# Two-layer graph network on one core: the sums right of the diagonal are turned back in sweep 2 and joined there with the own term and the bias

## The reference, cut to what matters

```python
# layer 0
d = sum(adj, axis=1); s0 = 1 / (sqrt(d) + 1e-8)
x1 = layernorm(x + (adj * s0[:, None] * s0[None, :]) @ (x @ W0 + b0))
# layer 1
adj_hat = adj + eye; s1 = 1 / sqrt(sum(adj_hat, axis=1))
out = layernorm(x1 + relu((adj_hat * s1[:, None] * s1[None, :]) @ (x1 @ W1) + b1))
```

## Time and profile before

| | before |
|---|---|
| median of 3 runs (lowest, highest) | 1765.88 us (1765.54, 1769.53) |
| the profiled execution, its own time | 1766.01 us |
| its span | 1764.2 us |
| TensorE (PE) busy | 1651.8 us, 94% |
| VectorE (DVE) busy | 1057.1 us, 60% |
| ScalarE (ACT) busy | 751.1 us, 43% |
| GpSimd (POOL) busy | 148.7 us, 8% |
| granted TensorE clock, mean | 0.991 of full speed |

### The profile page before, as it was taken

How to read it: one execution, slowest core, us unless ns; L and a number is a source line. 1 busy time by engine, 2 the same in 40 slices (tenths; PEclk the granted TensorE clock), 3 DMA queues, 4 the chain that set the end, 5 groups by cost and what they waited for, 6 DMA issues and landing times.

```text
span 1764.2 us, 25751 instructions
## 1 busy us (share of the span) xinstructions
PE 1651.8 (94%) x10392; PEld 1475.7 (84%) x10392; DVE 1057.1 (60%) x1837; ACT 751.1 (43%) x900; POOL 148.7 (8%) x171
## 2 busy tenths in 40 slices
PE   0688989999999999989999999999999999999996
PEld 0678989999999999977888888888888888888885
DVE  2233234344444455487666666555556899999996
ACT  4332322232111000046455454445445777777773
POOL 0000000000000000121100000000001011111111
PEclk9999999999999999999999999999999999999998
DMA  9999999999999876347676766556566999999991
GB/s 385 421 420 421 420 421 411 420 414 421 401 409 386 328 301 255 111 171 292 247 268 238 251 248 240 208 221 240 202 236 280 420 419 419 399 386 388 393 397 68
DMA packets 85462, 572.41 MB, mean 324 GB/s; under 512 B 10304, under 2 KB 10560, under 8 KB 19808
## 3 DMA queue, kind: packets, MB, share of 16 engines
q1 hardware_dynamic: 76320, 541.23, 77.1%
q0 software_dynamic: 9024, 29.54, 4.6%
HBM read 556.03 MB, written 14.70 MB: 324 GB/s over the span
## 4 chain that ended last, share of the span: by engine, by line
PE 85%; DVE 6%; issue 3%; DMA 2%; ACT 1%; SPq 1%; POOL 0%; ACTq 0%; DVEq 0%; POOLq 0%
PE acc L742 37%; PE acc L775 15%; PE acc L777 15%; PE acc L776 15%; DVE low L897 3%; DMA lent<-adj_far 1%; SPq L593 1%; PE mixed L677 1%; ACT high L794 1%; DVE stats L875 1%; PE turned L686 1%; PE mixed L713 1%; PE acc L765 1%; DVE z L1056 0%; DMA x_in<-x_rows 0%
## 5 line engine op out<-in xcount | busy, mean ns | idle before, releaser
L775 PE MATMUL acc<-high,feat_high 128*128 128x512 f32 x1336 | 529.9, 397 | 6.9 <-DVE low L897 6.8
L777 PE MATMUL acc<-high,feat_low 128*128 128x512 f32 x1336 | 523.1, 392 | 0.0
L776 PE MATMUL acc<-low,feat_high 128*128 128x512 f32 x1336 | 522.9, 391 | 0.0
L897 DVE TENSOR_TENSOR low<-own,high 128x1024 fp32r<-128x1024 f32 x330 | 390.4, 1219 | 174.0 <-ACT high L794 172.4
L794 ACT CAST high<-own 128x1024 fp32r<-128x1024 f32 x330 | 335.6, 1052 | 173.9 <-PE acc L777 153.6
L742 PE MATMUL acc<-feat,lent 128*128 128x129 f32 x2880 | 334.1, 275 | 20.2 <-issue 13.8
L742 PEld LDWEIGHTS acc<-feat,lent 128*128 128x128 f32 x2880 | 327.5, 192 | 22.4 <-issue 15.8
L775 PEld LDWEIGHTS acc<-high,feat_high 128*128 128x128 f32 x1336 | 251.7, 188 | 63.0 <-issue 11.3
L777 PEld LDWEIGHTS acc<-high,feat_low 128*128 128x128 f32 x1336 | 251.3, 188 | 55.1
L776 PEld LDWEIGHTS acc<-low,feat_high 128*128 128x128 f32 x1336 | 251.7, 188 | 51.5
L897 DVE TENSOR_TENSOR low<-lent,high 128x1024 fp32r<-128x1024 f32 x182 | 211.8, 1218 | 8.4 <-ACT high L794 6.4
(11 more groups left out here) (90 smaller groups left out, 765.6 us busy)
## 6 DMA issues: line engine op xcount, KB each, us to landing
own<-adj_tiles SPq DMA_DIRECT2D x205, 1024.0 KB, 7.3
lent<-adj_tiles SPq DMA_DIRECT2D x181, 1024.0 KB, 11.0
lent_h<-adj_tiles SPq DMA_DIRECT2D x48, 1024.0 KB, 11.1
lent<-adj_far SPq DMA_DIRECT2D x41, 1024.0 KB, 15.7
own<-adj_far SPq DMA_DIRECT2D x20, 1024.0 KB, 13.8
lent_h<-adj_far SPq DMA_DIRECT2D x17, 1024.0 KB, 13.5
x_in<-x_rows POOLq DMA_DIRECT2D x32, 256.0 KB, 6.3
x_t<-x_cols SPq DMA_DIRECT2D x16, 256.0 KB, 10.9
```

The source lines that it names most:

```text
L775: nc.tensor.matmul(bank, f_high, a_high[:, chunk], start=(u == plan.first[g] and q == 0), stop=False)
L776: nc.tensor.matmul(bank, f_high, a_low[:, chunk], start=False, stop=False)
L777: mm = nc.tensor.matmul(bank, f_low, a_high[:, chunk], start=False, stop=(u == plan.last[g] and q == Q - 1))
L897: nc.vector.tensor_tensor(low(m), raw(n)[:, half * HALF:(half + 1) * HALF], high(m).bitcast(F32), ALU.subtract).then_inc(low_ready, 1)
```

## The change

- The own term leaves TensorE: VectorE makes `skip = scale_sq * mixed + b1` right behind `features1_low` of the row (new `add_own`; `scale_sq` is made once). The matmuls of L765 and the identity for them are gone.
- The right sums are not stored. TensorE turns them from `stage` into `turned` (new `turn_right`, 4 transposes), and VectorE adds them, scaled, to `skip` (new `add_right`). GpSimd's queue stores `skip` (`store_skip`, 16 times where 15 sums were stored) and loads it in sweep 3.
- `empty_left1` becomes a copy on ScalarE. `add_x1` adds `skip_in` instead of the bias.
- `AHEAD` of sweep 3 becomes 2, `turn_out` comes two takes later, `make_out` one take later.
- New waits: `turn0` waits for all `skip` of earlier rows, `turn1` for `own_added` of the rows before it.

```diff
-AHEAD = {1: 0, 2: 1, 3: 1}
+AHEAD = {1: 0, 2: 1, 3: 2}
...
+        self.turn_right = {i: max(self.features1[i] + 1, self.last[("right1", i)] + 2) for i in range(NB - 1)}
...
-            self.turn_out[i] = self.empty[g] + 1
+            self.turn_out[i] = self.empty[g] + 3
...
-            (act if g[0] in ("late0", "right1") else dve).append(
-                ((hi_key if g[0] in ("late0", "right1") else lo_key)(k, 1), "empty_" + g[0], g[1]))
-            if g[0] == "right1":
-                pool.append(((k, 2, 0), "store_right1", g[1]))
+            act.append((hi_key(k, 1), "empty_" + g[0], g[1]))
...
+            dve.append((lo_key(k2, 9), "add_own", i))
+            if i < NB - 1:
+                dve.append((lo_key(self.turn_right[i], 2), "add_right", i))
+            pool.append(((self.turn_right.get(i, k2 + 1), 6, 0), "store_skip", i))
...
-            act.append((hi_key(k + 2, 5), "make_out", i))
+            act.append((hi_key(k + 3, 5), "make_out", i))
...
+                if kind == "store_skip":
+                    pool.wait_ge(skip_ready, up(i) + 1)
+                    pool.dma_start(skip_rows[i], skip[:, up(i) % 2]).then_inc(skip_stored[up(i) % 2], 16)
...
                     elif kind == "turn0":
                         pe.wait_ge(h_ready, up(i))
+                        pe.wait_ge(skip_ready, up(i))
...
                             pe.wait_ge(feat1_ready, up(i))
+                            pe.wait_ge(own_added, up(i))
...
+                    elif kind == "turn_right":
+                        m = stage_at[("empty_right1", i)]
+                        pe.wait_ge(h_ready, up(i) + 1)
+                        pe.wait_ge(skip_ready, up(i))
+                        pe.wait_ge(staged, m + 1)
+                        for q in range(Q):
+                            mm = nc.tensor.transpose(turned_q[:, q, :], stage[:, m % 2, q * P:(q + 1) * P], ident[:, :])
+                        mm.then_inc(turn_right_done, 1)
...
-                    if half == 1 and u == plan.last.get(("left1", i)):
-
-                        bank = acc[plan.bank[("left1", i)]]
-                        for q in range(Q):
-                            for f in (feat_high[1], feat_low[1]):
-                                nc.tensor.matmul(bank[:, q * P:(q + 1) * P], f[:, i * Q + q, :], ident_r[:, :],
-                                                 start=False, stop=False,
-                                                 skip_group_check=True)
...
+                elif kind == "empty_left1":
...
+                    nc.scalar.copy(y_t[:, m % 2, :], acc[b][:, :]).then_inc(bank_emptied[b], 1)
...
+                elif kind == "add_own":
...
+                    if up(i) >= 2:
+                        dve.wait_ge(skip_stored[r], 16 * (up(i) // 2))
+                    dve.wait_ge(mixed1_done, up(i) + 1)
+                    for q in range(Q):
+                        ins = nc.vector.scalar_tensor_tensor(
+                            out=skip[:, r, q, :], in0=mixed_q[:, q, :], scalar=scale_sq[:, i, q:q + 1],
+                            in1=b_sb[:, :], op0=ALU.mult, op1=ALU.add)
+                    ins.then_inc(own_added, 1)
...
+                elif kind == "add_right":
+                    r = up(i) % 2
+                    dve.wait_ge(own_added, up(i) + 1)
+                    dve.wait_ge(turn_right_done, stage_at[("empty_right1", i)] + 1)
+                    for q in range(Q):
+                        ins = nc.vector.scalar_tensor_tensor(
+                            out=skip[:, r, q, :], in0=turned_q[:, q, :], scalar=scale[:, i, 1, q:q + 1],
+                            in1=skip[:, r, q, :], op0=ALU.mult, op1=ALU.add)
+                    ins.then_inc(skip_ready, 1)
```

More of the change, by code:

```diff
@@ L178, in __init__ @@
             self.features1[i] = min(self.turn1[i] + FEATURES1_LAG, need)
+        self.turn_right = {i: max(self.features1[i] + 1, self.last[("right1", i)] + 2) for i in range(NB - 1)}
+        assert all(self.turn_right[i] <= self.turn0[i - 1] for i in range(1, NB - 1) if i - 1 in self.late_rows)
         self.empty = {g: u + 1 for g, u in self.last.items()}
@@ L186, in __init__ @@
                 self.empty[g] = max(self.empty[g], self.turn_out[ROWS3[m - 2]])
-            self.turn_out[i] = self.empty[g] + 1
+            self.turn_out[i] = self.empty[g] + 3
             if m >= 1:
                 self.turn_out[i] = max(self.turn_out[i], self.turn_out[ROWS3[m - 1]] + 2)
-        for table, kind in ((self.turn0, "turn0"), (self.turn1, "turn1"), (self.features1, "features1")):
+        for table, kind in ((self.turn_right, "turn_right"), (self.turn0, "turn0"), (self.turn1, "turn1"),
+                            (self.features1, "features1")):
             for i in reversed(range(NB)):
-                if kind != "turn0" or i in self.late_rows:
+                if i in table and (kind != "turn0" or i in self.late_rows):
                     self.pe_before.setdefault(min(table[i], self.end), []).append((kind, i))
@@ L448, in gnn_kernel @@
         ident = put("ident", [P, P])
-        ident_r = put("ident_r", [P, P], F32R)
+        skip = put("skip", [P, 2, Q, P])
+        scale_sq = put("scale_sq", [P, NB, Q])
         ones = put("ones", [P, 1])
@@ L522, in gnn_kernel @@
         staged = sem("staged")
-        sums_stored = [sem(f"sums_stored{r}") for r in range(2)]
+        scale_sq_ready = sem("scale_sq_ready")
+        turn_right_done = sem("turn_right_done")
+        own_added = sem("own_added")
+        skip_ready = sem("skip_ready")
+        skip_stored = [sem(f"skip_stored{r}") for r in range(2)]
         sums0_ready = sem("sums0_ready")
@@ L563, in ring_of_x1 @@
             before = ring_of_x(0 if up(0) % 2 == r else 1)[1]
-            loaded = sum(16 * (2 if k != NB - 1 else 1) for k in ROWS3[:third[i] + 1] if third[k] % 2 == r)
+            loaded = sum(32 for k in ROWS3[:third[i] + 1] if third[k] % 2 == r)
             return r, before + loaded
@@ L831, in _ @@
                     act.sem_inc(sums0_ready, 1)
+                elif kind == "empty_left1":
+                    g = ("left1", i)
+                    b, m = plan.bank[g], third[i]
+                    act.wait_ge(halves_used, 2 * plan.last[g] + 2)
+                    if m >= 2:
+                        act.wait_ge(turn_out_done, m - 1)
+                    nc.scalar.copy(y_t[:, m % 2, :], acc[b][:, :]).then_inc(bank_emptied[b], 1)
+                    act.wait_ge(bank_emptied[b], plan.bank_turn[g] + 1)
+                    act.sem_inc(y_t_ready, 1)
                 elif kind == "make_out":
@@ L837, in _ @@
                     else:
-                        for r in range(2):
-                            act.wait_ge(sums_stored[r], 16 * len([k for k in stage_at.values() if k % 2 == r]))
+                        act.wait_ge(turn_right_done, NB - 1)
                     for q in range(Q):
@@ L978, in _ @@
                     ins.then_inc(feat0_ready, 1)
+                    if i == NB - 1:
+                        nc.vector.tensor_tensor(scale_sq[:, :, :], scale[:, :, 1, :], scale[:, :, 1, :],
+                                                ALU.mult).then_inc(scale_sq_ready, 1)
                 elif kind == "split_low":
@@ L1098 @@
     args.append(nc.dram_tensor("x1_rows", (NB, P, Q, P), F32, kind="Internal").ap())
-    args.append(nc.dram_tensor("sums_rows", (NB, P, T), F32, kind="Internal").ap())
+    args.append(nc.dram_tensor("skip_rows", (NB, P, Q, P), F32, kind="Internal").ap())
     args.append(nc.dram_tensor("nat_rows", (SPILLED, P, Q, W), F32, kind="Internal").ap())
```

49 lines of the change are left out of this document (15 added, 34 removed).

## The result

| | before | changed |
|---|---|---|
| median of the runs | 1767.13 us (6 runs, 1765.54 to 1771.34) | 1775.5 us (6 runs, 1772.75 to 1778.78) |
| ratio to before, with its 95% interval | | 1.0049 (1.0039 to 1.0059) |
| the profiled execution, and its span | 1766.01 us, 1764.2 | 1777.69 us, 1775.9 |
| granted TensorE clock, mean | 0.991 | 0.982 |

The six runs of before include the three known earlier. The change makes the kernel 8.4 us (0.5%) slower, where 10.1 was forecast.

What follows compares the result with a forecast made beforehand. TensorE bounds sweeps 2 and 3, except sweep 2's start, bound by a chain through GpSimd's load, VectorE and a tile load. 10.3 + 7.5 + 4.8 - 14.2 + 1.0 + 0.7 = +10.1 on 1766.0 gives 1776.1 us, range 1766.5 to 1783.

Steps and rivals of the forecast that it cites:

- A: Start of sweep 2: new VectorE blocks and the late load of x for row 11 cost +10.3 us.
- B: Sweep 2, turns of rows 11 and 10 at one place: TensorE waits for add_right of row 11, +7.5 us.
- C: Sweep 2: eleven new turns of right sums on TensorE at 0.44 us each, +4.8 us.
- D: Mostly sweep 3: own term off TensorE, 16 blocks of 0.89 us, -14.2 us.
- E: Sweep 3: left sums on ScalarE cost nothing; add_x1's new waits for make_out at the new places cost +1.0 us.
- the distance between the two stays: Sweep 3: VectorE's relief keeps its distance to TensorE, so TensorE's waits for lows stay roughly 4.2 us.
- F: The kernel's end: the copy, then make_out of row 8, delay VectorE's last add_x1, +0.7 us.
- Short load, clock holds: Start of sweep 2: load lands in 3.1 us, clock does not fall; +3.2, 1769.2 us, chance 0.17.
- Faster, hidden: Start of sweep 2: new VectorE work is hidden; -7.6, 1758.4 us, chance 0.08.
- Sweep 3 does not follow: Sweep 3: tiles or lows come late and half the gain is lost; +17, 1783 us, chance 0.12.
- What would show it: Profile signs: two sweep 2 TensorE waits, about 5 and 4 us, half clock behind; load at 798; sweep 3 13 us shorter.

Runs made afterwards that it cites:

- experiment 1: Changed kernel with GpSimd's stores of skip put behind the load of x of the same place: 1770.65 us, ratio 1.0016.
- experiment 3: Kernel before with only the load of x for row 11 moved later, behind the store of row 12's right sums: 1776.66 us, ratio 1.0054.
- experiment 4: Kernel before without the own term's 8 small matmuls per row in sweep 3 (left out of the result): 1759.94 us, ratio 0.9958.
- experiment 7: Experiment 4 with the left sums copied by ScalarE at the old places, right sums also left out: 1761.06 us, ratio 0.9965.
- experiment 9: Experiment 4 with the change's places in sweep 3 (AHEAD 2, later turn_out and make_out), VectorE still joining sums: 1755.65 us, ratio 0.9931.
- experiment 6: Experiment 5 with make_out one take earlier, at k + 2 as before the change: 1758.73 us, ratio 0.9954.
- experiment 12: Experiment 4 with only turn_out two takes later: 1758.6 us, ratio 0.995.
- experiment 11: Changed kernel with AHEAD of sweep 3 back to 1, its other places as changed: 1773.72 us, ratio 1.0033.
- experiment 10: Experiment 7 with the change's places in sweep 3 (AHEAD 2, later turn_out and make_out): 1754.46 us, ratio 0.9926.
- experiment 5: Changed kernel with skip stores behind the load of x and add_right of row 11 directly behind add_own: 1763.08 us, ratio 0.9975.
- experiment 2: Changed kernel with add_right of row 11 directly behind add_own, ahead of the low of take 193 and split_low: 1769.68 us, ratio 1.0014.

## Why the prediction was right, and where its sizes were off

The forecast was 1776.1 us and slower; measured were 1775.5 and +0.5%. The times lie nearer together than the changes do, by luck: the sum was 1.7 us too high (+10.1 for +8.4), and it was laid on an execution 1.1 us below the median that the kernel before now has. By its steps:

**A, the load of x behind the store.** Forecast +10.3, measured +9.0. The load was to be issued at 797.9; less the 2.9 us of sweep 1 it was, at 798.1. Its length was taken as 6.3 us and was 7.0, and TensorE waited 5.3 instead of 4.8. Those two made A larger. Two other terms made it smaller. The clock: seven matmuls started 0.43 us apart instead of 0.23, from 812.44 to 815.56, and from 816 on the granted clock was 1.00. That is 3.1 us at half clock and not 5.6, so 1.5 us and not 2.8. And the old waits it swallowed: besides the 1.84 us at 814.2 there is one of 0.19, and by the starts of the matmuls around them the two cost 2.3, not 1.8. Experiments 1 and 3 show the mechanism from both sides: load forward -7.0, load back in the old kernel +8.0. Both are differences of single executions; the ratios of all runs say -5.8 and +9.5.

**B, two turns at one place.** Forecast +7.5, measured +6.6. The wait was 4.18 for 4.3. The clock was at 0.50 from 848 to 853 and at 0.94 in the next us, so some 5.1 us at half clock and not 5.6, which takes 0.3 off. What was left out: before, TensorE had a wait of 0.39 there too, some 0.5 by the starts around it, which the new one swallows. These three make up the difference.

**C, eleven turns.** Forecast +4.8, measured +4.5 to the turn of row 0 and 0.44 for that one: 5.0.

**D and E, sweep 3.** Together -13.2 forecast, -12.9 measured (-12.5 and the 0.44 of row 0). The number was right, its reasoning was not, and that it came out is luck: a gain was booked in full for a reason that does not hold, and the moves that did bring it out were booked as a cost. (The prediction also set the last of the 16 blocks apart; all 16 stand ahead of the last big matmul, which leaves the sum as it is.) The prediction said that TensorE's 0.89 us a row are gained because VectorE is rid of 0.70 as well. Experiment 4 showed that without any help only 6.3 of 14.2 come out, experiment 7 that the copy on ScalarE is no help by itself, and experiment 9 that the places in the lists are: `turn_out` later, and the lead with `make_out` later. The prediction weighed these moves only as a cost (+1.0, the new wait of `add_x1` for `make_out`, which is in the trace as 2.7 us in two waits; the trace names "issue", and experiment 6, with `make_out` back, has neither). The step that did not hold is "the distance between the two stays": with only the own term gone (experiment 4) TensorE waits 7.4 us for lows and not 4.2, and for the left sums as well. Put side by side, by lead and place of `make_out`:

| lead, `make_out` | sweep 3, us | ScalarE's wait for `shift`, us |
|---|---|---|
| 1, take k+2: before; experiments 4, 7, 12 | 396.4; 390.1, 392.5, 388.3 | 35.1; 41.1, 39.6, 41.0 |
| 1, k+3: experiment 11 | 384.3 | 6.5 |
| 2, k+3: changed; 9, 10 | 384.0; 383.5, 382.0 | 3.9; 4.9, 4.0 |
| 2, k+2: experiment 6 | 378.8 | 23.4 |

The 396.4 of before still has the own term in it; of the others, all with the old pair are slower than all with one of the two moved. That agrees with this reading: `make_out` waits in ScalarE's list with highs behind it, and with a lead of one take TensorE feels that; a later place ends the wait, and a larger lead makes it harmless, since in experiment 6 ScalarE stands 23.4 us and the sweep is the shortest. The kernels of the table differ in more than this pair (`turn_out` stands later in all of the last three lines and, of the first, in experiment 12 alone), and the clock fell in sweep 3 of experiment 7 and the changed kernel twice, of 4, 9, 10 and 12 once, of 6, 11 and before not at all, at some 1.6 us each. So this reading is argued from them and not shown by one edit. In the trace of before the row was there, and I passed over it as idle time of an engine with room:

```profile
ACT o L841 <- DVE shift L1071: 35.1, 15, 3.4
```

**F, the end.** Forecast +0.7, measured +1.2. From the start of the last big matmul to VectorE's last `add_x1` it was 1.99 us before and should be 2.67; it is 2.93 (L1082 at 1761.78, behind the `make_out` that began at 1760.03). The remaining 0.2 lie behind it and can't be told from noise. Experiments 6 and 11 both take the 1.1 us back.

**The rivals.** *Short load, clock holds*: no; the load took 7.0 and the clock fell at both places. The estimate of 2.6 us by the Trainium skill ("DMA: Bandwidth & Descriptors", "Anatomy of one DMA") is far from 7.0 here, and the trace disagrees with it for this load. It agrees for one that has no tiles beside it: the load issued at 755.9 us in the changed kernel took 2.66. *Faster, hidden*: its deciding point, the low of take 185 before 800 us, came at 811. Experiment 5 comes near to this rival: with the load issued early and `add_right` moved ahead it is faster than before, 1763.08. But even there the low of take 185 starts at 805.7, since the new blocks still stand ahead of it, and not before 800; so the rival's 1758.4 is not reached. *Sweep 3 does not follow*: it did, but experiment 4 shows how near that was. Half the gain lost, as that rival had it, is what happens without the moved places.

**What would show it**: L765 is gone, the load is at 798 (less the 2.9), TensorE is idle 5.3 us at 807 to 812 and 4.2 before a turn of `late_t`, each with half clock behind it, and sweep 3 is some 13 us shorter, all as stated. The second wait came 36 us after the first and not 20 to 30; I had not moved it by A's own delay.

## What to carry to other kernels

A load queued behind a store waits for whatever the store waits for: before a store of a late result is put into a queue, look which loads stand behind it and which engine stands for them (some 6 to 7 us here, and one sort key takes them back). When an engine is relieved of work, look whether the in-order lists of the engines that feed it hold a wait ahead of what it needs, even where those engines have idle time; here more than half of the gain stayed in until entries of these lists were moved. A right total is no proof of its parts: only taking the own term out alone showed that this one rested on places that the sum had booked as a cost.

## What the runs showed of the hardware that was not expected

**The clock also fell after shorter idle stretches.** In sweep 3 of the changed kernel TensorE waits 1.96 us up to 1442.6 and 1.95 up to 1490.9, and each time about eight matmuls at half clock follow:

```profile
1440.00:1443.00 3.00, 1.04 (x5) 0.58 (x4) 2.93 (x11) 1.71 (x2) 1.59 (x1) 1.00 0.99 414
1443.00:1446.00 3.00, 3.00 (x10) 2.39 (x9) 3.00 (x5) 2.32 (x5) 0.71 (x2) 0.60 1.03 433
```

After 1.8 us it had stayed, after 4.2 and 5.3 it fell each time. By the starts of the matmuls, the waits for lows and their clock cost 7.4 us in the changed kernel and 5.0 before, at nearly the same sum of waits. In experiment 6, whose longest is 1.1, nothing of the kind is seen.

But such a wait does not always bring the clock down. Experiment 5 has the same order in sweep 3 and the same two waits of 1.95 us. Behind the first the clock stayed, and its sweep 3 took 382.3 us, where the changed kernel and experiments 1 and 2, in which it fell twice, took 384.0, 384.0 and 383.9:

```profile
1434.00:1437.00 3.00, 3.00 (x14) 2.44 (x14) 3.00 (x5) 2.16 (x5) 0.71 (x2) 1.00 1.00 418
```

In the 14 profiled executions, from 690 us to the end of sweep 3, the shortest wait of TensorE with half clock behind it is 1.89 us (experiment 9) and the longest with none is 2.88 (experiment 2). Every one of 3.8 us or more had it.

**Where it falls differs between executions.** The 2.9 us at the end of sweep 1 go with two places, at the same matmuls in the same order, with TensorE idle 2.5 us (the first) and 3.8 (the second) in both. (Half clock is the level of 1.2 GHz.) In the changed kernel's execution:

```profile
697.00:707.00 10.00, 8.15 (x58) 8.16 (x59) 2.98 (x13) 0.00 (x0) 0.00 (x0) 0.83 0.01 3
719.00:735.00 16.00, 12.21 (x84) 12.12 (x83) 6.78 (x23) 0.00 (x0) 1.64 (x1) 0.79 0.20 67
```

and in that of the kernel before:

```profile
697.00:707.00 10.00, 7.86 (x70) 7.86 (x71) 3.68 (x17) 0.00 (x0) 0.00 (x0) 1.00 0.00 2
719.00:735.00 16.00, 12.26 (x97) 12.26 (x98) 7.33 (x27) 0.00 (x0) 2.63 (x2) 0.89 0.14 58
```

Over all 14 profiled executions the clock fell behind the first wait in 8, and `features1` of row 15 began between 761.9 and 765.8 us. This is as large as the spread of 3 us around either median, and likely a part of it; only profiled executions show it, so that is argued, not shown. It is why spans of two profiles (11.7 apart) say less of a change than marks inside one sweep.

**The same load takes very different times.** The load of x for row 11 took 8.4 us in the kernel before, 7.0 in the changed one, and 4.1 in experiment 3, with the same 256 KB from the same queue. That is not only its place. Experiments 4, 7, 9, 10 and 12 have the order of before up to the end of sweep 2, and there it took 7.3, 6.9, 10.3, 9.4 and 9.1; experiment 11 has the change's, and there it took 5.6. So a forecast of this load can't be better than some 2 us either way. Issued before 794 us it took 6.9 to 10.3 in all executions, issued after 800 it took 4.1 to 7.0. What runs beside it was not varied by itself, so what sets the length is open.
